# A transformer block with two expert layers: where the first expert's rows are transposed, and how the chunk ahead of it is emptied

## The chip, the cores and the metric

The kernel runs on one core of one Trainium2 chip. The metric is the device time of one execution in microseconds (us). A core has five engines with queues of their own: TensorE (PE in the profile; its weight loads are shown as PEld), VectorE (DVE), ScalarE (ACT), GpSimd (POOL) and SyncE (SP), which here only issues transfers. Engines wait for one another through semaphores.

## The reference

The input is 4096 tokens of 256 numbers. The block is a feed-forward layer (FFN) at half weight, an attention layer, and the same FFN once more:

```
x = x + 0.5 * ffn(layernorm(x))
x = x + attention(layernorm(x))
x = x + 0.5 * ffn(layernorm(x))

# ffn, on its input r:
a       = layer_norm(r, attn_nw, attn_nb)
combine, dispatch = top1_gate(a, wg, capacity=512)     # 8 experts, one per token
expert  = gelu(dispatched(a) @ inter_w[e] + inter_b[e]) @ output_w[e] + output_b[e]
dense   = gelu(a @ res_inter_w + res_inter_b) @ res_output_w + res_output_b
coef    = softmax(a @ res_coef)
return dense * coef[0] + combined(expert) * coef[1] + r
```

An expert takes at most 512 tokens, the first ones that chose it. All of it is float32.

## The kernel before

**Tiling.** Tokens are worked on in chunks of 512 (four tiles of 128). Both kinds of MLP, the dense one on a chunk of tokens and an expert's on its 512 slots, are one routine, `Mlp` with `tensor_chunk`: for each of 8 slices `k` of the 1024 inner features there is `up(k)` (6 matmuls of 512 columns), GELU on ScalarE, written twice (`f_h` and the rounded `f_h_hi`), a subtraction on VectorE that makes the low part `f_h_lo` (`split_h`, L311), and `down(k)` (12 matmuls of 256 columns into four accumulators `f_down`). Every float32 operand is split into a high and a low part, and three products stand for one. `down` runs two slices behind `up`, so TensorE's order is up(k), down(k-2), up(k+1), down(k-1), and so on; at a chunk's end stand up(7), down(5), down(6), down(7), and at its beginning up(0), up(1), up(2), down(0), up(3).

**Order of the chunks.** In the first FFN six dense chunks are followed by the 8 experts and then by two dense chunks, in the second FFN seven dense chunks by the 8 experts and one dense chunk. The order on each engine is the order in which the Python program writes it. What is done beside a slice is given as a dictionary from `k` to a list of functions (`beside`); on VectorE they follow `split_h(k)`, on ScalarE the GELU of slice k, on TensorE `down(k)`. The key `EARLY` on TensorE stands just ahead of up(2).

**Towards the experts.** During the fourth dense chunk (`mlp(3, ...)` on VectorE) each token's expert and slot are found: `choose`, `choose_one`, `place`, then `address` (six small instructions, the row addresses) and `weigh` (three, the gate's weight). After `weigh` GpSimd scatters all tokens to `slots_in` in memory with 32 indirect transfers (L580). When all have landed, SyncE loads the first expert's rows from there (`load_rows`, L397). VectorE reads their marks (`tokens_of`, L858 to L864), and TensorE transposes them (`turn_slots`, L1067, 8 small matmuls into `f_side`). ScalarE applies gain and shift (`slots_T`, L972, `f_aT`), and VectorE splits the result into `f_x_hi` (L273) and `f_x_lo` (L278), with which the expert's up(0) can begin. An expert's weights come as float32 and are split by VectorE, one slice at a time (`split_w`, L848 to L852, four instructions a slice), four slices ahead of use; for the first expert `first_weights(0)` to `first_weights(3)` are the first four. TensorE waits at each up(k) for the split of slice k.

**Emptying a chunk.** `empty` adds the bias to the four accumulators into the buffer `f_part` (L666) and adds `f_part`, scaled, to the tokens in `x_all` (L671). down(0) of the next chunk waits for the first of the two and for `split_h(0)`.

Of the kernel before, what the change touches and what calls it, by code (L numbers as in the profile page):

```python
# [35 lines left out]
NC = TOKENS // CH  # L36
# [363 lines left out]
def ffn_programs(nc, ctx, sems, mem, layer, x_tiles, x_in, res_w1, res_w2, res_b2, inter_w, output_w, output_b, slots_in,  # L400
# [3 lines left out]
    first_late = NC - LATE[layer]  # L404
# [7 lines left out]
    m = Mlp(nc, ctx, sems, tag)  # L412
# [196 lines left out]
    def vector(dve, beside=None, constants=None):  # L609
# [41 lines left out]
        def mix_of(a):  # L651

            dve.wait_ge(s["th_ready"], a + 1)
            v.tensor_scalar(c0[:, bass.ds(a * TT, TT)], th[:], 0.25, 0.25, ALU.mult, ALU.add)
            v.tensor_scalar(c1[:, bass.ds(a * TT, TT)], th[:], -0.25, 0.25, ALU.mult, ALU.add)

        def empty(c, turn):

            if turn > c:

                dve.wait_ge(s["stored"], 16 * TT * NE)
            if turn == 0:
                dve.wait_ge(s["b2_in"], 16)
            dve.wait_ge(m.down_done, turn * NK + NK)
            for t in range(TT):
                i = v.tensor_tensor(part[:, t, :], m.down_ps[t][:, 0:D], b2[:], ALU.add)  # L666
            i.then_inc(m.evacuated, 1)
            dve.wait_ge(m.evacuated, turn + 1)
            dve.wait_ge(s["x_made"], c + 1)
            for t in range(TT):  # L670
                i = v.scalar_tensor_tensor(x_all[:, c * TT + t, :], part[:, t, :], c0[:, c * TT + t:c * TT + t + 1],  # L671
                                           x_all[:, c * TT + t, :], ALU.mult, ALU.add)
            i.then_inc(s["updated"], 1)
# [31 lines left out]
        def rows_T(c):  # L705
            return aT_all[:, NC - 1 - c]

        def mlp(c, beside=None, turn=None):
            turn = c if turn is None else turn
            for k in range(NK):  # L710
                if k == NK - 1:
                    dve.wait_ge(s["aT_all_ready"], c + 2)
                    m.split_x_hi(dve, turn + 1, rows_T(c + 1))
                m.split_h(dve, turn, k, turn == 0)
                if k == NK - 1:
                    m.split_x_lo(dve, turn + 1, rows_T(c + 1))
                for f in (beside or {}).get(k, ()):
                    f()
            empty(c, turn)

        def mlp_before_experts(c, beside, after):

            for k in range(NK):
                m.split_h(dve, c, k, False)
                for f in beside.get(k, ()):
                    f()
            dve.wait_ge(s["e_aT_ready"], 1)
            m.split_x_hi(dve, c + 1, aT[:])
            m.split_x_lo(dve, c + 1, aT[:])
            for f in after:  # L730
                f()
            empty(c, c)

        def mlp_last(beside):
            for k in range(NK):
# [8 lines left out]
        def norms(c):  # L744

            a, b, d = c * 3 + 1, c * 3 + 2, c * 3 + 3
            at = {0: [lambda: stats_of(a)], 2: [lambda: logits_of(d - 3), lambda: y_of(a)], 3: [], 4: [],
                  5: [lambda: logits_of(a)], 6: [lambda: mix_of(d - 3)]}
            if c:
                at[0].insert(0, lambda: mix_of(a - 3))  # L750
                at[4].append(lambda: mix_of(b - 3))
            if b < NC:
                at[3].append(lambda: stats_of(b))
                at[4].append(lambda: y_of(b))
                at[5].append(lambda: stats_of(d))
                at[7] = [lambda: logits_of(b), lambda: y_of(d)]
            else:
                at[7] = [lambda: logits_of(NC)]
            return at
# [72 lines left out]

        mlp(1, norms(1))
        mlp(2, norms(2))
        mlp(3, {0: [lambda: mix_of(NC - 1), choose], 1: [choose_one], 3: [place], 4: [address], 5: [weigh]})
        for c in range(4, first_late - 1):
            mlp(c)

# [15 lines left out]
        def tokens_of(e):  # L854

            dve.wait_ge(feed.rows_in, (e + 1) * 16)
            marks = feed.rows[:, :, D]
            v.tensor_copy(weight[:], feed.rows[:, :, D + 1])  # L858
            v.tensor_scalar(vacant[:], marks, 0.0, None, ALU.is_equal).then_inc(s["token_chain"], 1)
            dve.wait_ge(s["token_chain"], e * 2 + 1)  # L860
            v.scalar_tensor_tensor(vacant[:], mem["spare"][:, 0:TT], 1.0, vacant[:], ALU.add,
                                   ALU.mult).then_inc(s["token_chain"], 1)
            dve.wait_ge(s["token_chain"], e * 2 + 2)
            v.scalar_tensor_tensor(token[:], marks, -1.0, vacant[:], ALU.add, ALU.add).then_inc(s["token_read"], 1)  # L864

        def expert(e, parity, first=False, last=False):
            c = e + first_late
            for k in range(NK):
                if k == 4:
                    dve.wait_ge(s["token_read"], e + 1)  # L870
                    if not first:
                        dve.wait_ge(s["stored"], e * 16 * TT)
                    v.tensor_copy(weight_now[:], weight[:])
                    v.tensor_copy(to[:], token[:]).then_inc(s["to_ready"], 1)
                    if not last:
                        dve.wait_ge(s["to_ready"], e + 1)
                        tokens_of(e + 1)
                following = rows_T(first_late) if last else aT[:]
                if k == NK - 1:
                    if not last:  # L880
                        dve.wait_ge(s["e_aT_ready"], e + 2)
                    m.split_x_hi(dve, c + 1, following)
                m.split_h(dve, c, k, False)
                if k == NK - 1:
                    m.split_x_lo(dve, c + 1, following)
                if not (last and k + W_AHEAD >= NK):

                    if not (first and k + W_AHEAD < W_RING):
                        dve.wait_ge(m.down_done, c * NK + (k + W_AHEAD - W_RING + 1))
                    split_w(e, k + W_AHEAD)  # L890
            dve.wait_ge(m.down_done, c * NK + NK)
            dve.wait_ge(eb2_in[parity], (e - parity) * 8 + 16)
            for t in range(TT):
                i = v.tensor_tensor(part[:, t, :], m.down_ps[t][:, 0:D], eb2[:, parity, :], ALU.add)
            i.then_inc(m.evacuated, 1)
            dve.wait_ge(m.evacuated, c + 1)
            for t in range(TT):
                i = v.tensor_scalar(part[:, t, :], part[:, t, :], weight_now[:, t:t + 1], None, ALU.mult)
            i.then_inc(s["done_ready"], 1)

        def first_weights(k):
            if k == 0:
                dve.wait_ge(s["scattered"], 16 * NT)
            split_w(0, k)

        mlp_before_experts(first_late - 1, {6: [lambda: first_weights(0), lambda: tokens_of(0)], 7: [lambda: first_weights(1)]},
                           [lambda: first_weights(2), lambda: first_weights(3)])
        expert(0, 0, first=True)
        with dve.Fori(0, NE // 2 - 1) as i:
            expert(i * 2 + 1, 1)  # L910
            expert(i * 2 + 2, 0)
# [76 lines left out]
    def tensor(pe, beside=None, constants=None):  # L988
# [72 lines left out]
        def turn_slots(e, first=False):  # L1061
            pe.wait_ge(feed.rows_in, (e + 1) * 16)
            if not first:
                pe.wait_ge(s["e_aT_ready"], e)
            for kd in range(KD):
                for t in range(TT):
                    i = nc.tensor.transpose(m.side[kd][:, t * P:(t + 1) * P], feed.rows[:, t, kd * P:(kd + 1) * P],  # L1067
                                            mem["id32"][:])
            i.then_inc(s["e_turned"], 1)
# [6 lines left out]
                return (lambda kd: ew1[0][:, r, kd, :]), (lambda kd: ew1[1][:, r, kd, :]), ew2[0][:, r, :], ew2[1][:, r, :]  # L1076
            m.tensor_chunk(pe, e + first_late, expert_weights, False, None if last else {EARLY: lambda: turn_slots(e + 1)})

        m.tensor_chunk(pe, first_late - 1, weights, False, {6: lambda: turn_slots(0, True)})
        with pe.Fori(0, NE - 1) as e:  # L1080
            expert(e)
        expert(NE - 1, last=True)
        for c in range(first_late, NC):
            m.tensor_chunk(pe, c + NE, weights, False, (beside or {}).get(c), last_layer and c == NC - 1)

    return Programs(sync, gpsimd, vector, scalar, tensor, s, m)


# [693 lines left out]
```

## Time and profile before

| | us |
|---|---|
| three runs: median | 1217.13 |
| three runs: lowest to highest | 1215.64 to 1217.16 |
| the profiled execution's own time | 1215.53 |
| its span (first to last instruction) | 1213.8 |
| TensorE busy with matmuls | 1175.2 (97%) |
| VectorE busy | 901.7 (74%) |
| ScalarE busy | 686.2 (57%) |
| GpSimd busy | 273.4 (23%) |

The profiled execution was 1.6 us faster than the median of the three runs, and its time is 1.7 us longer than its span. Times of instructions below are counted from the span's start. The dense chunk ahead of the first expert ends at 166 us in the first FFN and at 998 us in the second.

### The profile page before, as it was taken

What the parts mean: (1) busy time and instruction counts of PE and PEld (TensorE: products, weight loads), DVE (VectorE), ACT (ScalarE), POOL (GpSimd) and SP (SyncE); (2) the same over time, 40 slices, a digit from 0 to 9 for tenths busy, and PEclk for the clock granted to TensorE, in tenths of its full rate; (3) what the DMA queues carried; (4) which work ended last, traced back from release to release, by engine and by line L of the source; (5) the groups of instructions that cost most, each with busy time, mean ns of one, the idle gap of its engine ahead of it and who ended that gap; (6) DMA issues with size and microseconds to landing.
All of it is one profiled execution on the core that took longest, in us unless ns stands there. A gap on an engine that the chain in (4) does not pass through costs nothing. (4 is left out here: it accounts for less than half of the span.)

```text
span 1213.8 us, 28464 instructions
## 1 busy us (share of the span) xinstructions
PE 1175.2 (97%) x11133; PEld 874.6 (72%) x11133; DVE 901.7 (74%) x1963; ACT 686.2 (57%) x998; POOL 273.4 (23%) x322
## 2 busy tenths in 40 slices
PE   7999999999999989999999999978999999999998
PEld 6888889999989744434353443437888888999987
DVE  6867468888867877878779877567866459788874
ACT  4554445445454567786867778755455445554443
POOL 4651711121131000000000000014624600322422
PEclk9999999999999999999999999999999999999999
DMA  9702224344203633230442121007103514555622
GB/s 284 210 1 98 99 93 160 123 150 159 91 31 94 101 67 63 43 65 2 88 72 45 28 41 32 2 14 184 36 26 106 174 53 147 129 154 132 137 56 53
DMA packets 144992, 110.58 MB, mean 91 GB/s; under 512 B 73132, under 2 KB 132856, under 8 KB 144888
## 3 DMA queue, kind: packets, MB, share of 16 engines
q1 hardware_dynamic: 135672, 92.27, 29.0%
q0 software_dynamic: 9216, 16.85, 6.0%
q8 instruction: 74, 1.21, 0.4%
q14 instruction: 30, 0.25, 0.1%
HBM read 57.59 MB, written 34.73 MB: 76 GB/s over the span
## 5 line engine op out<-in xcount | busy, mean ns | idle before, releaser
L301 ACT ACTIVATE f_h<-f_up,vecT 128x512 f32<-128x512 f32 x256 | 176.5, 689 | 379.5 <-PE f_up L290 370.9
L1538 ACT ACTIVATE a_probs<-a_S 128x1024 f32<-128x1024 f32 (+3 forms) x320 | 272.9, 900 | 68.5 <-PE a_S L1431 35.0
L311 DVE TENSOR_TENSOR f_h_lo<-f_h,f_h_hi 128x512 fp32r<-128x512 f32 x256 | 176.2, 690 | 136.2 <-ACT f_h_hi L301 135.6
L1721 DVE TENSOR_TENSOR a_probs<-a_probs 128x2048 f32<-128x2048 f32 (+2 forms) x78 | 147.5, 1891 | 39.9 <-ACT a_probs L1538 37.9
L301 ACT ACTIVATE f_h_hi<-f_up,vecT 128x512 fp32r<-128x512 f32 x256 | 174.7, 682 | 0.0
L322 PE MATMUL f_down<-f_ew_hi,f_h_hi 128*128 128x256 f32 x512 | 143.3, 280 | 3.3 <-DVE f_h_lo L311 3.3
L322 PE MATMUL f_down<-f_w_hi,f_h_hi 128*128 128x256 f32 x512 | 145.3, 284 | 0.7 <-DVE f_h_lo L311 0.7
L1448 PE MATMUL a_cx<-a_probs,a_V 128*32 128x512 f32 (+3 forms) x1280 | 144.7, 528 | 0.4 <-DVE a_dd L1699 0.4
L324 PE MATMUL f_down<-f_w_hi,f_h_lo 128*128 128x256 f32 x512 | 144.8, 283 | 0.0
L323 PE MATMUL f_down<-f_w_lo,f_h_hi 128*128 128x256 f32 x512 | 144.7, 283 | 0.0
L323 PE MATMUL f_down<-f_ew_lo,f_h_hi 128*128 128x256 f32 x512 | 142.9, 279 | 0.0
L324 PE MATMUL f_down<-f_ew_hi,f_h_lo 128*128 128x256 f32 x512 | 142.6, 278 | 0.0
L1427 PE MATMUL a_S<-a_QT,a_early_keys 128*32 128x512 f16 (+3 forms) x1792 | 122.8, 359 | 3.5 <-ACT a_probs L1538 3.5
L1427 PEld LDWEIGHTS a_S<-a_QT,a_early_keys 128*32 128x32 f16 x1792 | 40.2, 95 | 93.2 <-ACT a_probs L1538 44.4
L322 PEld LDWEIGHTS f_down<-f_ew_hi,f_h_hi 128*128 128x128 f32 x512 | 96.3, 188 | 8.4 <-DVE f_h_lo L311 4.1
L322 PEld LDWEIGHTS f_down<-f_w_hi,f_h_hi 128*128 128x128 f32 x512 | 97.9, 191 | 5.5 <-DVE f_w_lo L769 1.5
L323 PEld LDWEIGHTS f_down<-f_w_lo,f_h_hi 128*128 128x128 f32 x512 | 97.7, 191 | 3.8
L323 PEld LDWEIGHTS f_down<-f_ew_lo,f_h_hi 128*128 128x128 f32 x512 | 96.1, 188 | 4.4
L324 PEld LDWEIGHTS f_down<-f_w_hi,f_h_lo 128*128 128x128 f32 x512 | 97.7, 191 | 0.0
L324 PEld LDWEIGHTS f_down<-f_ew_hi,f_h_lo 128*128 128x128 f32 x512 | 96.2, 188 | 0.0
L290 PE MATMUL f_up<-f_x_hi,f_w_hi 128*128 128x512 f32 x256 | 86.0, 417 | 6.0 <-DVE f_x_hi L273 4.9
L580 POOL DMA_INDIRECT slots_in<-f_y_all,f_scatter_at x64 | 66.9, 1046 | 75.0 <-issue 75.0
(201 smaller groups left out, 2168.4 us busy)
## 6 DMA issues: line engine op xcount, KB each, us to landing
f_aT_all<-in_L_ffn_inter_w SPq DMA_DIRECT2D x32, 512.0 KB, 4.0
f_aT_all<-in_L_ffn_output_w SPq DMA_DIRECT2D x32, 512.0 KB, 4.9
slots_in<-f_zeros SPq DMA_DIRECT2D x16, 516.0 KB, 13.2
f_aT_all<-slots_in SPq DMA_DIRECT2D x16, 516.0 KB, 4.3
out<-x_all SPq DMA_DIRECT2D x9, 512.0 KB, 3.4
x_all<-in_L_attn_x SPq DMA_DIRECT2D x8, 512.0 KB, 9.5
moe_rows<-f_zeros SPq DMA_DIRECT2D x8, 512.0 KB, 8.5
a_moe<-moe_rows SPq DMA_DIRECT2D x6, 512.0 KB, 4.2
```

Of the source, the lines that this page charges most:

```text
L290: last = nc.tensor.matmul(bank[:], w(kd), xs[:, kd, :], start=(n == 0), stop=(n == 3 * KD - 1))
L301: i = self.nc.scalar.activation(to, self.up_ps[k % UP_BANKS][:], ACT.Gelu_apprx_tanh, bias=bias)
L311: nc.vector.tensor_tensor(lo, h, hi, ALU.subtract).then_inc(self.h_split, 1)
L322: nc.tensor.matmul(bank, hi, w2_hi, start=(k == 0), stop=False)
L323: nc.tensor.matmul(bank, hi, w2_lo, start=False, stop=False)
L324: last = nc.tensor.matmul(bank, lo, w2_hi, start=False, stop=(k == NK - 1))
L580: nc.gpsimd.indirect_dma_start(out=slots_in, out_offset=bass.IndirectOffsetOnAxis(ap=scatter_at[:, t:t + 1], axis=0), in_=y_all[:, t, :], ...
L1427: last = nc.tensor.matmul(S[hp][k:k + DH, i, lo:CH], KT[j // TT][:, h, j % TT * P + k:j % TT * P + k + DH], QT[:, c % 2, h, lo:CH], start= ...
L1448: last = nc.tensor.matmul(cx[G % 2][i * DH:(i + 1) * DH, lo:CH], V[:, v_tile(b * QC, j), h * DH:(h + 1) * DH], probs[:, q % P_RING, i, lo: ...
L1538: nc.scalar.activation(probs[:, q % P_RING, hp * 2:hp * 2 + 2, lo:CH], S[hp][:, :, lo:CH], ACT.Exp).then_inc(exp_done[hp], 1)
L1721: v.tensor_tensor(total, total, probs[:, (q + 1) % P_RING, :, lo:CH], ALU.add).then_inc(s["summed"], 1)
```

## The change

There are three edits, and all of them act in both FFNs.

1. On TensorE `turn_slots(0)`, the transposition of the first expert's rows, stands behind down(5) of the dense chunk ahead of it and no longer behind down(6).
2. On VectorE the emptying of that chunk is cut in two parts, `take` (the accumulators into `f_part`) and `put` (`f_part` into `x_all`), and both stand inside the first expert. Slice 0 there is now: `first_weights(2)`, `take`, `split_h(0)`, `first_weights(3)`, `split_w(0, 4)`. `put` stands ahead of `split_h(2)`. For the other chunks `empty` calls both in one go, as it was.
3. `weigh` follows `address` directly, beside slice 4 of the fourth chunk; it stood beside slice 5.

```diff
         def empty(c, turn):
+            take(c, turn)
+            put(c, turn)
+
+        def take(c, turn):
             if turn > c:
                 dve.wait_ge(s["stored"], 16 * TT * NE)
...
             for t in range(TT):
                 i = v.tensor_tensor(part[:, t, :], m.down_ps[t][:, 0:D], b2[:], ALU.add)
             i.then_inc(m.evacuated, 1)
+
+        def put(c, turn):
             dve.wait_ge(m.evacuated, turn + 1)
             dve.wait_ge(s["x_made"], c + 1)
...
-        def mlp_before_experts(c, beside, after):
+        def mlp_before_experts(c, beside):
...
             m.split_x_hi(dve, c + 1, aT[:])
             m.split_x_lo(dve, c + 1, aT[:])
-            for f in after:
-                f()
-            empty(c, c)
...
-        mlp(3, {0: [lambda: mix_of(NC - 1), choose], 1: [choose_one], 3: [place], 4: [address], 5: [weigh]})
+        mlp(3, {0: [lambda: mix_of(NC - 1), choose], 1: [choose_one], 3: [place], 4: [address, weigh]})
...
         def expert(e, parity, first=False, last=False):
             c = e + first_late
             for k in range(NK):
+                if first and k == 0:
+                    first_weights(2)
+                    take(c - 1, c - 1)
+                if first and k == 2:
+                    put(c - 1, c - 1)
...
                 m.split_h(dve, c, k, False)
+                if first and k == 0:
+                    first_weights(3)
...
-        m.tensor_chunk(pe, first_late - 1, weights, False, {6: lambda: turn_slots(0, True)})
+        m.tensor_chunk(pe, first_late - 1, weights, False, {5: lambda: turn_slots(0, True)})
```

The order on VectorE from the first expert's `f_x_hi` on, before (`f_ew_hi` and `f_ew_lo` are a slice of the expert's weights, `f_b` is the bias, `f_c` a token's coefficient):

```order
L273 CAST f_x_hi<-f_aT 128x1024
L278 TENSOR_TENSOR f_x_lo<-f_aT,f_x_hi 128x1024
L848 CAST f_ew_hi<-f_aT_all 128x256
L849 CAST f_ew_hi<-f_aT_all 128x256
L851 TENSOR_TENSOR f_ew_lo<-f_aT_all,f_ew_hi 128x256
L852 TENSOR_TENSOR f_ew_lo<-f_aT_all,f_ew_hi 128x256
L848 CAST f_ew_hi<-f_aT_all 128x256
L849 CAST f_ew_hi<-f_aT_all 128x256
L851 TENSOR_TENSOR f_ew_lo<-f_aT_all,f_ew_hi 128x256
L852 TENSOR_TENSOR f_ew_lo<-f_aT_all,f_ew_hi 128x256
L666 TENSOR_TENSOR f_part<-f_down,f_b 128x256 x4
L671 SCALAR_TENSOR_TENSOR x_all<-f_part,f_c,x_all 128x256 x4
L311 TENSOR_TENSOR f_h_lo<-f_h,f_h_hi 128x512
```

The same place of the changed kernel, up to the same first `f_h_lo` of the expert:

```order
L273 CAST f_x_hi<-f_aT 128x1024
L278 TENSOR_TENSOR f_x_lo<-f_aT,f_x_hi 128x1024
L852 CAST f_ew_hi<-f_aT_all 128x256
L853 CAST f_ew_hi<-f_aT_all 128x256
L855 TENSOR_TENSOR f_ew_lo<-f_aT_all,f_ew_hi 128x256
L856 TENSOR_TENSOR f_ew_lo<-f_aT_all,f_ew_hi 128x256
L670 TENSOR_TENSOR f_part<-f_down,f_b 128x256 x4
L311 TENSOR_TENSOR f_h_lo<-f_h,f_h_hi 128x512
```

One slice of weights and the four instructions into `x_all` are gone from ahead of the first `f_h_lo`. They stand behind it: the slice of weights at once, the four instructions (now L677) behind two more slices of weights and the second `f_h_lo`, as the next rows show.

The order on VectorE of the changed kernel a little further on, from the second `f_h_lo` to the third:

```order
L311 TENSOR_TENSOR f_h_lo<-f_h,f_h_hi 128x512
L852 CAST f_ew_hi<-f_aT_all 128x256
L853 CAST f_ew_hi<-f_aT_all 128x256
L855 TENSOR_TENSOR f_ew_lo<-f_aT_all,f_ew_hi 128x256
L856 TENSOR_TENSOR f_ew_lo<-f_aT_all,f_ew_hi 128x256
L677 SCALAR_TENSOR_TENSOR x_all<-f_part,f_c,x_all 128x256 x4
L311 TENSOR_TENSOR f_h_lo<-f_h,f_h_hi 128x512
```

Before, nothing stood there between the slice of weights and the third `f_h_lo`.

The order on TensorE at the end of the dense chunk, changed kernel, from the last of down(5) to the first of down(6) (`f_side` takes the transposed rows):

```order
L322 MATMUL f_down<-f_w_hi,f_h_hi 128x256
L323 MATMUL f_down<-f_w_lo,f_h_hi 128x256
L324 MATMUL f_down<-f_w_hi,f_h_lo 128x256
L1077 MATMUL f_side<-id,f_aT_all 128x128 x8
L322 MATMUL f_down<-f_w_hi,f_h_hi 128x256
L323 MATMUL f_down<-f_w_lo,f_h_hi 128x256
```

Before, the row of the 8 transposing matmuls (L1067 there) stood 12 matmuls later, between down(6) and down(7).

## Rows read from the trace of the kernel before

**Rows 1.** The page, 40 slices of the span: TensorE's granted clock in tenths.

```profile
PEclk9999999999999999999999999999999999999999
```

**Rows 2.** Chain that ended last, second FFN: start, us, what.

```profile
1002.95 1.34 DVE f_part L666 x4
...
1005.99 0.61 DVE f_h_lo L311
```

**Rows 3.** Timeline of TensorE, second FFN: start, us, instruction, count [idle before <-releaser].

```profile
996.05 1.04 PE L1067 MATMUL f_side<-id,f_aT_all 128*128 128x128 f32 x8
...
998.24 0.28 PE L324 MATMUL f_down<-f_w_hi,f_h_lo 128*128 128x256 f32 x1
999.35 0.73 PE L290 MATMUL f_up<-f_x_hi,f_ew_hi 128*128 128x512 f32 x2 [0.83 <-DVE f_x_hi L273]
...
1001.18 0.63 PE L290 MATMUL f_up<-f_x_hi,f_ew_hi 128*128 128x512 f32 x2
...
1002.58 1.04 PE L1067 MATMUL f_side<-id,f_aT_all 128*128 128x128 f32 x8
1003.37 0.71 PE L290 MATMUL f_up<-f_x_hi,f_ew_hi 128*128 128x512 f32 x2
...
1006.64 0.39 PE L322 MATMUL f_down<-f_ew_hi,f_h_hi 128*128 128x256 f32 x1 [1.64 <-DVE f_h_lo L311]
...
1008.16 0.63 PE L290 MATMUL f_up<-f_x_hi,f_ew_hi 128*128 128x512 f32 x2
```

**Rows 4.** Timeline of TensorE, first FFN.

```profile
163.69 1.04 PE L1067 MATMUL f_side<-id,f_aT_all 128*128 128x128 f32 x8
...
165.88 0.28 PE L324 MATMUL f_down<-f_w_hi,f_h_lo 128*128 128x256 f32 x1
...
175.81 0.63 PE L290 MATMUL f_up<-f_x_hi,f_ew_hi 128*128 128x512 f32 x2
```

**Rows 5.** Timeline of VectorE, first FFN.

```profile
166.25 0.69 DVE L273 CAST f_x_hi<-f_aT 128x1024 fp32r<-128x1024 f32 x1 [1.35 <-ACT f_aT L972]
166.98 1.23 DVE L278 TENSOR_TENSOR f_x_lo<-f_aT,f_x_hi 128x1024 fp32r<-128x1024 f32 x1
168.12 0.29 DVE L848 CAST f_ew_hi<-f_aT_all 128x256 fp32r<-128x256 f32 x1
...
170.52 1.41 DVE L666 TENSOR_TENSOR f_part<-f_down,f_b 128x256 f32<-128x256 f32 x4
171.96 1.67 DVE L671 SCALAR_TENSOR_TENSOR x_all<-f_part,f_c,x_all 128x256 f32<-128x256 f32 x4
173.55 0.68 DVE L311 TENSOR_TENSOR f_h_lo<-f_h,f_h_hi 128x512 fp32r<-128x512 f32 x1
174.16 0.29 DVE L848 CAST f_ew_hi<-f_aT_all 128x256 fp32r<-128x256 f32 x1
```

**Rows 6.** Timeline of ScalarE, first FFN.

```profile
164.77 1.45 ACT L972 ACTIVATE f_aT<-f_side,vecT 128x512 f32<-128x512 f32 x2 [2.48 <-PE f_side L1067]
169.30 0.69 ACT L301 ACTIVATE f_h<-f_up,vecT 128x512 f32<-128x512 f32 x1 [3.08 <-PE f_up L290]
```

**Rows 7.** Timeline of VectorE, first FFN: the marks of the loaded rows are read.

```profile
162.45 0.17 DVE L858 COPY f_weight<-f_aT_all 128x4 f32<-128x4 f32 x1 [1.06 <-DMA f_aT_all<-slots_in]
```

**Rows 8.** Line L397, the loads of an expert's rows.

```profile
DMA to landing us min/median/max: 3.6/4.3/6.8
```

**Rows 9.** Timeline of VectorE, fourth chunk of the first FFN.

```profile
111.20 0.68 DVE L311 TENSOR_TENSOR f_h_lo<-f_h,f_h_hi 128x512 fp32r<-128x512 f32 x1
111.81 0.41 DVE L829 TENSOR_REDUCE f_t<-f_ex 128x32 f32<-128x256 f32 x1
...
117.30 1.22 DVE L278 TENSOR_TENSOR f_x_lo<-f_aT_all,f_x_hi 128x1024 fp32r<-128x1024 f32 x1
```

**Rows 10.** Timeline of GpSimd, first FFN: three of the 32 scatters.

```profile
113.80 1.24 POOL L580 DMA_INDIRECT slots_in<-f_y_all,f_scatter_at  x1 [27.97 <-issue]
...
116.62 0.96 POOL L580 DMA_INDIRECT slots_in<-f_y_all,f_scatter_at  x1 [0.30 <-issue]
117.88 1.48 POOL L580 DMA_INDIRECT slots_in<-f_y_all,f_scatter_at  x1 [0.30 <-issue]
```

More of the change, by code:

```diff
@@ L904, in first_weights @@
             split_w(0, k)
-        mlp_before_experts(first_late - 1, {6: [lambda: first_weights(0), lambda: tokens_of(0)], 7: [lambda: first_weights(1)]},
-                           [lambda: first_weights(2), lambda: first_weights(3)])
+        mlp_before_experts(first_late - 1, {6: [lambda: first_weights(0), lambda: tokens_of(0)], 7: [lambda: first_weights(1)]})
         expert(0, 0, first=True)
```

## The prediction

> **What bounds the kernel now.** I began with the page: TensorE is busy for 97% of the span, and its clock is granted in full, the 2.4 GHz level, in every slice [rows 1]. So the time is TensorE's work plus the few stretches in which it stands still, and a change that leaves its matmuls as they are can only add or remove such stretches. The waits of TensorE name them; the chain that ended last shows the same ones as stretches in which it leaves TensorE. It leaves it around the first expert of an FFN: transposed rows, ScalarE, `f_x_hi`, `f_x_lo`, two slices of weights, the emptying of the accumulators, the update of `x_all`, `f_h_lo`, and only then back to a `down` matmul [rows 2]. I then read both engines' timelines there.
>
> Second FFN [rows 3]: the last matmul of the dense chunk starts at 998.24. These matmuls start every 0.12 us, so TensorE is free at 998.36, and up(3) of the expert starts at 1008.16, 9.80 us later. Its own work between the two is up(0), up(1), up(2), down(0) and one transposition of the second expert's rows. An `up` takes 1.40 (1001.18 to 1002.58), the transposition 0.79 (1002.58 to 1003.37), and `down` 12 x 0.12, about 1.40. That is 4 x 1.40 + 0.79 = 6.39, and 3.41 is idle:
> - up(0) starts 999.35 - 998.36 = 0.99 late, for `f_x_hi`;
> - up(0) takes 1001.18 - 999.35 = 1.83 instead of 1.40, since its fifth matmul waits for `f_x_lo`: 0.43;
> - down(0) would start at 1003.37 + 1.40 = 1004.77 and starts at 1006.64, for `f_h_lo`: 1.87. Of this I leave 0.08 for slower first weight loads behind the transposition, which stay;
> - down(0) then takes 1.52, a restart of 0.12.
>
> That is 3.33 us to be had. First FFN [rows 4]: from 165.88 + 0.12 = 166.00 to 175.81 it is 9.81, the same picture, 3.34 us. Both together are 6.67 us.
>
> **The change part by part.** I work it out in the first FFN, where everything is tightest.
>
> The transposition, one place sooner. TensorE's own sum is unchanged: 8 matmuls move across 12 others. They start at 163.69 - 12 x 0.12 = 162.25. Everything behind them moves by the same 1.44: ScalarE's two activations from 164.77 to 163.33 [rows 6], with 1.45 us of duration; it is free then, since it had been idle for 2.48 before them. `f_x_hi` moves from 166.25 to 164.81; VectorE was idle for 1.35 before it [rows 5], and the work ahead of it comes up to 0.6 sooner (below), so 1.44 is there. `f_x_hi` ends at 165.50, half a microsecond before TensorE is free at 166.00: the 0.99 is gone. `f_x_lo` starts 0.73 later (166.98 - 166.25), at 165.54, and ends at 166.77. The fifth matmul of up(0) comes at 166.00 + 4/6 x 1.40 = 166.93: the 0.43 is gone too, with 0.16 to spare.
>
> The emptying in two parts. Before the first `f_h_lo` of the expert there now stand, from 165.54 on: `f_x_lo` 1.14 (166.98 to 168.12), one slice of weights 1.20 (two of them take 168.12 to 170.52) and `take` 1.44 (170.52 to 171.96) [rows 5]. `f_h_lo` can start at 169.32. Its other input is ScalarE's: up(0) ends at 167.40, and the first GELU started 0.46 after up(1) (169.30 [rows 6]; up(1) at 168.84 by the same offset as 1001.18 in rows 3), so the pair runs from 167.86 to about 169.1. So `f_h_lo` is done at 169.32 + 0.68 = 170.00. TensorE gets to down(0) at 166.00 + 3 x 1.40 + 0.79 + 0.08 = 171.07. The 1.87 and the restart are gone, with a microsecond to spare. down(0) also waits for `take`, done at 169.3.
>
> What is displaced. VectorE then does a slice of weights (`first_weights(3)`, to 171.13; up(3) needs it at about 172.5), another (to 172.33), `f_h_lo` 1 (0.61, 173.55 to 174.16, so to 172.94; down(1) needs it at 173.9), a slice (174.14), `put` (1.59, 171.96 to 173.55, so to 175.73), `f_h_lo` 2 (done by 176.4; down(2) comes at 172.5 + 3 x 1.40 = 176.7). This is the narrowest place, 0.3 us. Behind it VectorE has 1.20 + 0.61 = 1.81 us of work for each 2.80 us of TensorE's and catches up by a microsecond a slice. Nothing is done twice: I cost it at 0, and at up to 0.6 in each FFN if the cover is gone there (0.3 of margin and as much again). Below zero it can't be.
>
> What else hangs on these. The second expert's rows are requested when the first one's are turned. TensorE came to them 1002.58 - 997.09 = 5.5 us after the first turn's end [rows 3] and now comes 5.4 after it, and did not wait; of all such loads the median is 4.3 and the longest 6.8 [rows 8]. Cost 0, at most 1.4. SyncE's load of the second expert's weights waits for the fourth split slice, which was done at 170.5 in the first FFN and now is at 171.1; it is wanted at slice 4, ten microseconds later. In the second FFN SyncE's store of the chunk waits for `put`, two microseconds later than now; behind it are queued the second half of those weights, which wait for the eighth split slice and so go later still. Cost 0.
>
> The rows for the earlier turn. The wait that edit 1 adds is TensorE's for the loaded rows, behind down(5), with down(6), down(7) and the whole expert queued behind it. In the second FFN they have lain there for long. In the first they land just in time: VectorE waited 1.06 for them and read at 162.45 [rows 7], which is 0.2 later than the new turn at 162.25. Here edit 3 counts: `weigh` started at 111.81 behind a `split_h` at 111.20 [rows 9], and starts at 111.20 now, 0.61 sooner. GpSimd's scatters had waited for it [rows 10], so rows land at about 161.8, 0.4 before they are wanted. The `split_h` that `weigh` overtakes is 1.1 later and is not needed on TensorE for three more. Cost 0; 0.2 if the scatters take up the 0.61.
>
> The scatters are where a rule speaks against the change. The scatter that began at 117.88, inside an `f_x_lo` subtraction of 117.30 to 118.52, took 1.48 us, while the one at 116.62 took 0.96 [rows 9, 10]. The Trainium skill (SBUF — State Buffer, the section "SBUF: two separate sides") says that VectorE and GpSimd share a port pair as an exclusive lock, which an instruction of either holds to its end, and that a transfer issued by GpSimd then stands and waits for its descriptors. The pair at 117.88 agrees, 0.52 longer for 0.64 of overlap; by the rule a shifted train would meet other subtractions, and one more such meeting would eat 0.5 of the 0.61 and leave a wait of about 0.1 in the sum.
>
> **The sum.** 3.33 + 3.34 = 6.67, less 0 to 1.2 for `f_h_lo` 2. The profiled execution goes from 1213.8 to 1207.1 of span and from 1215.53 to 1208.9 of time. The median of the runs shown was 1.6 above the profiled execution, so I forecast 1217.13 - 6.7 = 1210.4. I take the near end, since every place has its margin worked out from durations that repeat to 0.02 us between the two FFNs.
>
> **Rivals.**
> - A, VectorE becomes the wait (12%). `f_x_hi` doesn't come sooner, because rows or ScalarE are late; only the emptying helps. Then 0.99 and 0.43 stay, and `f_h_lo` 0 is done at 166.25 + 0.73 + 1.14 + 1.20 + 1.44 + 0.68 = 171.44, before down(0) at 172.5. Gain 1.87 - 0.08 + 0.12 = 1.9 in each FFN, 3.8 in all: 1213.3. Against it: the idle time of ScalarE and VectorE in rows 5 and 6.
> - B, the gain is given back (5%): later stretches (experts, attention, the last chunk) hang on something that the first expert doesn't move, as a transfer. Time 1217.1. Against it: from there on the chain is almost all TensorE, and no transfer has a fixed time.
> - C, slower (4%). The scatters stretch in the first FFN, by their meeting VectorE's subtractions. Each could be 1.48 - 0.96 = 0.52 longer, 32 of them 16.6 us; rows then land up to 16.6 later, TensorE waits 16.6 - 0.4 = 16.2 at the turn, and the time is 1217.1 + 16.2 - 6.7 = 1226.6. It decides from 7.1 us of lateness on; by the nearest rows only some of the scatters are long.
> - D, the change removes less, as the turn waits up to 1.4 us for the second expert's rows in each FFN (4%): 1213.2.
>
> My forecast has 75%.
>
> **How the numbers follow.** Three runs of one kernel spread by 1.5 us, and about 0.2% (2.4 us) is what can be told from no change. Faster by more than that: forecast, A, and D, 75 + 12 + 4 less 1 for their tails = 90%. Within it: B, and 1 of the tails, 6%. Slower: C, 4%. The range begins at 1208.6: the whole gain below the lowest run (1215.64 - 6.7 = 1208.9) and a little for noise. It ends at 1213.6, which holds A and D.
>
> **What would show it.** The 8 transposing matmuls start 1.4 us sooner than at 163.7 and 996.0, and no wait stands before them. up(0) of the first expert follows down(7) with no idle time and takes 1.40. `f_part` is filled ahead of the first `f_h_lo`, and down(0) follows up(2) without a wait. From the dense chunk's last matmul to up(3) it is 6.5 us instead of 9.8 in each FFN. The first scatter starts at 113.2. I am wrong if TensorE waits at the turn in the first FFN for rows, at down(2) for `f_h_lo`, or if the distance from the first expert's up(3) to the span's end (1213.8 - 1008.2 = 205.6) grows.

## The result, and the profile after

The changed kernel takes 1211.38 us, the median of 6 runs (1209.9 to 1212.19), and the kernel before 1216.95 beside it (6 runs, 1215.64 to 1217.71). The ratio is 0.9951, with an interval of 0.994 to 0.9961. It is faster by 5.6 us, where 6.7 were forecast, and the time lies inside the range; the interval holds gains from 4.7 to 7.3 us. The profiled execution of the changed kernel took 1212.19 us, with a span of 1210.4 and a mean granted clock of 0.993; the one of before had 0.997. Two later runs of the kernel before, at 1465 and 1312 us with clocks of 0.75 and 0.85, were in a slow state and are left out of every number below.

The page of the changed kernel, busy times and the granted clock in 40 slices:

```profile
PE 1177.2 (97%) x11133; PEld 876.4 (72%) x11133; DVE 901.9 (75%) x1963; ACT 686.1 (57%) x998; POOL 272.6 (23%) x322
PEclk9999999999999999999999999988999999999999
```

Two slices show an 8 where [rows 1] has 9s. I come back to them; first the places that were changed. Timeline of TensorE, first FFN (start, us, instruction, count):

```profile
162.17 1.03 PE L1077 MATMUL f_side<-id,f_aT_all 128*128 128x128 f32 x8
165.81 0.28 PE L324 MATMUL f_down<-f_w_hi,f_h_lo 128*128 128x256 f32 x1
165.92 0.63 PE L290 MATMUL f_up<-f_x_hi,f_ew_hi 128*128 128x512 f32 x2
167.31 0.63 PE L290 MATMUL f_up<-f_x_hi,f_ew_hi 128*128 128x512 f32 x2
168.70 1.04 PE L1077 MATMUL f_side<-id,f_aT_all 128*128 128x128 f32 x8
169.50 0.71 PE L290 MATMUL f_up<-f_x_hi,f_ew_hi 128*128 128x512 f32 x2
170.97 0.28 PE L322 MATMUL f_down<-f_ew_hi,f_h_hi 128*128 128x256 f32 x1
...
172.37 0.63 PE L290 MATMUL f_up<-f_x_hi,f_ew_hi 128*128 128x512 f32 x2
```

No row has a wait behind it. The rows are turned at 162.17, 1.52 sooner than in [rows 4]. The dense chunk's last matmul is followed by up(0) after 0.11 us, up(0) takes 167.31 - 165.92 = 1.39, and down(0) comes 1.47 after up(2). From 165.81 + 0.12 to up(3) it is 6.44 us; 9.81 were read before and 6.5 forecast. The second FFN, against [rows 3]:

```profile
993.29 1.04 PE L1077 MATMUL f_side<-id,f_aT_all 128*128 128x128 f32 x8
...
996.92 0.28 PE L324 MATMUL f_down<-f_w_hi,f_h_lo 128*128 128x256 f32 x1
997.04 0.63 PE L290 MATMUL f_up<-f_x_hi,f_ew_hi 128*128 128x512 f32 x2
...
1003.49 0.63 PE L290 MATMUL f_up<-f_x_hi,f_ew_hi 128*128 128x512 f32 x2
```

1003.49 - 997.04 = 6.45: the same. Together the two places give (9.81 - 6.44) + (9.80 - 6.45) = 6.72 us. VectorE of the changed kernel in the first FFN, against [rows 5, 7]:

```profile
161.23 0.16 DVE L862 COPY f_weight<-f_aT_all 128x4 f32<-128x4 f32 x1
...
165.46 1.23 DVE L278 TENSOR_TENSOR f_x_lo<-f_aT,f_x_hi 128x1024 fp32r<-128x1024 f32 x1
...
167.80 1.41 DVE L670 TENSOR_TENSOR f_part<-f_down,f_b 128x256 f32<-128x256 f32 x4
169.13 0.68 DVE L311 TENSOR_TENSOR f_h_lo<-f_h,f_h_hi 128x512 fp32r<-128x512 f32 x1
...
173.94 1.67 DVE L677 SCALAR_TENSOR_TENSOR x_all<-f_part,f_c,x_all 128x256 f32<-128x256 f32 x4
175.52 0.68 DVE L311 TENSOR_TENSOR f_h_lo<-f_h,f_h_hi 128x512 fp32r<-128x512 f32 x1
```

The marks are read at 161.23 without a wait (162.45 before, after 1.06). The first `f_h_lo` is done at 169.81, 1.16 ahead of down(0); the third at 176.20, while down(2) would come at 172.37 + 3 x 1.40 = 176.57: 0.37 to spare, 0.3 forecast.

So the two places gave what was forecast, and yet this execution is only 1215.53 - 1212.19 = 3.34 us faster than the profiled one of before. Matching each matmul with its like, TensorE is ahead by 3.4 us behind the first FFN, by 1.8 from 451 on, by 1.3 at the second FFN's start, by 4.7 behind its first expert and by 3.4 at the end. Three stretches gave back 1.7, 0.4 and 1.3, and none of them lies where an edit was made.

### The profile page after: what moved, and what is told of

Its sections match the earlier page's. It is cut to its first block and busy times, and to the rows that moved or that the text cites. A ratio compares the mean times of both kernels' runs of the same rounds, so it can differ in the third digit from the quotient of the medians.

```text
span 1210.4 us, 28464 instructions
## 1 busy us (share of the span) xinstructions
PE 1177.2 (97%) x11133; PEld 876.4 (72%) x11133; DVE 901.9 (75%) x1963; ACT 686.1 (57%) x998; POOL 272.6 (23%) x322
```

## The experiments

All were compared with the kernel before on the same chip. Three questions were open: whether each edit is worth what its terms say, how near the margins are, and who takes 3.3 us back.

**The kernel before, once more.** No edit.

> The kernel before, unchanged, once more, for the spread of its own runs and their granted clocks. Theory 1 (stretches of half clock fall differently in each execution, behind the same idle stretches of TensorE): its mean clock differs from run to run between about 0.992 and 0.997, and the runs with the lower clock are the longer ones, by 1 to 3 us; the profile of before, with 0.997 and 1215.53 us, was a lucky one. Rival (the change costs clock): every run of this kernel has 0.996 or more, while the changed kernel has 0.992 to 0.994.

1216.58 us, 11 runs; ratio 0.9995 (0.9986 to 1.0004). As the theory has it, the clocks go from 0.993 to 0.997, and the two runs at 0.993 are the longest (1217.91 and 1218.21), the four at 0.997 lie from 1215.82 to 1216.58. Its profile loses 0.7 over the experts of the second FFN against the profile of before, with the same code. Part of what is given back is thus a difference between executions.

**The earlier turn alone.**

```diff
-        m.tensor_chunk(pe, first_late - 1, weights, False, {6: lambda: turn_slots(0, True)})
+        m.tensor_chunk(pe, first_late - 1, weights, False, {5: lambda: turn_slots(0, True)})
```

> The kernel before with the first edit alone: the first expert's rows transposed behind down(5). Everything on VectorE from f_x_hi on moves by 1.44 us in each FFN, so 0.99 and 0.43 of idle time go, but the first f_h_lo still stands behind two slices of weights, f_part and x_all. Theory (the two edits add up): down(0) starts 1.44 sooner, gain 2.9 us in all, 1214.1 where before has 1217.0; TensorE waits about 1.8 us at down(0). Rival (the turn alone gives nothing, as the last wait is f_h_lo's with a fixed end): below 0.5 us.

1214.04 us, 8 runs; ratio 0.9973 (0.9963 to 0.9984). TensorE of this kernel, first FFN:

```profile
161.91 1.09 PE L1067 MATMUL f_side<-id,f_aT_all 128*128 128x128 f32 x8
...
172.57 0.39 PE L322 MATMUL f_down<-f_ew_hi,f_h_hi 128*128 128x256 f32 x1 [1.63 <-DVE f_h_lo L311]
```

The idle time ahead of up(0) is gone and the one ahead of down(0) stays. TensorE's lead over before grew by 1.33 us at the first place and by 1.45 at the second; the terms 0.99 + 0.43 say 1.42. In the first FFN TensorE lost 0.1 at the turn itself: VectorE, which waits for the same rows, read them at 161.89, and the turn started at 161.91.

**The emptying in two parts alone.** The changed kernel with the turn back behind down(6) and `weigh` back at slice 5.

```diff
-  {... 4: [address, weigh]}          {5: lambda: turn_slots(0, True)}
+  {... 4: [address], 5: [weigh]}     {6: lambda: turn_slots(0, True)}
```

> The second edit alone: the emptying in two parts and the later fourth slice of weights, the turn behind down(6) and the gate's weight at slice 5 as before. Theory: 0.99 and 0.43 of idle time stay at up(0), the wait at down(0) of 1.8 us goes: gain 1.9 us in each FFN, 3.8 in all, 1213.2. Rival (VectorE has no slack behind): some of it comes back at down(1) or down(2), gain below 2.5.

1214.47 us, 9 runs; ratio 0.9973 (0.9963 to 0.9982). The places gave 1.92 each, 1.9 forecast. The two edits add up: 1.33 + 1.92 and 1.45 + 1.92 are within 0.1 of the 3.36 us that both places gave in the changed kernel. The median is 2.6 us below before, not 3.8. The profiled execution (1215.54 us) shows 1.7 of loss near 425 and 1.4 over the late experts.

**`weigh` back at slice 5,** the rest as changed.

```diff
-  4: [address, weigh]
+  4: [address], 5: [weigh]
```

> The changed kernel without its third edit: the gate's weight is made beside slice 5 again. Theory: the scatters of the first FFN start 0.6 us later, rows land at about 161.8 where the turn comes at 162.2, so nothing or up to 0.3 us is lost: 1211.4 to 1211.7. Rival (the third edit is what makes the rows arrive in time): TensorE waits 0.5 us or more at the turn of the first FFN and the time is 1212 or more.

1210.84 us, 5 runs; ratio 0.9945 (0.9931 to 0.9958), beside 0.9949 (0.9934 to 0.9963) for the changed kernel, run again. Edit 3 brings nothing that the times can show; what it does to the scatters comes next.

**The changed kernel again.**

> The changed kernel once more, as the partner of the others of this group. Theory (the gain is 6.7 us in every pair of executions with equal mean clock, and the 1.1 us that the first measurement lacked came from its clocks): about 1210.2 with a mean clock of 0.994 to 0.997 and about 1212.0 with 0.993, against about 1217.0 and 1218.0 for the kernel before. Rival (the change itself costs 1 us later on): 1211.4 whatever the clock.

1210.64 us, 5 runs: 1209.84 to 1210.64 at a clock of 0.994, 1211.38 and 1211.69 below it, as the theory has it. The scatters, by line (operation, count | busy us, mean ns | idle before): of before, of the changed kernel's first profile, and of its second:

```profile
L580 POOL DMA_INDIRECT slots_in<-f_y_all,f_scatter_at x32 | 33.4, 1044 | 37.4 <-issue 37.4
```
```profile
L580 POOL DMA_INDIRECT slots_in<-f_y_all,f_scatter_at x32 | 32.8, 1024 | 36.8 <-issue 36.8
```
```profile
L580 POOL DMA_INDIRECT slots_in<-f_y_all,f_scatter_at x32 | 34.0, 1062 | 36.8 <-issue 36.8
```

The first scatter starts at 113.80, 113.09 and 113.28. With `weigh` back it is 113.85, and the row is that of before. The changed kernel's second profile began 0.5 sooner than before and spent 0.6 more in the scatters. Its rows were just in time; VectorE and TensorE there:

```profile
162.25 0.17 DVE L862 COPY f_weight<-f_aT_all 128x4 f32<-128x4 f32 x1 [0.78 <-DMA f_aT_all<-slots_in]
```
```profile
162.32 1.04 PE L1077 MATMUL f_side<-id,f_aT_all 128*128 128x128 f32 x8
```

0.07 us of margin and no wait, in place of the 0.4 forecast. The six profiles taken with `weigh` at slice 5 show 33.4 each, the seven with it at slice 4 show 32.7 or 32.8 four times and 34.0 three times. The difference is made at one scatter, the fourth, which starts together with an `f_x_lo` subtraction. The two rows in the changed kernel's first profile, and in its second:

```profile
117.21 0.96 POOL L580 DMA_INDIRECT slots_in<-f_y_all,f_scatter_at  x1 [0.30 <-issue]
117.19 1.28 DVE L278 TENSOR_TENSOR f_x_lo<-f_aT_all,f_x_hi 128x1024 fp32r<-128x1024 f32 x1
```
```profile
117.41 2.02 POOL L580 DMA_INDIRECT slots_in<-f_y_all,f_scatter_at  x1 [0.30 <-issue]
117.38 1.22 DVE L278 TENSOR_TENSOR f_x_lo<-f_aT_all,f_x_hi 128x1024 fp32r<-128x1024 f32 x1
```

In all four short trains that scatter starts 0.020 to 0.025 us behind `f_x_lo` and takes 0.96, and the subtraction takes 1.28; in all three long ones it starts 0.034 to 0.039 behind and takes 2.01 or 2.02, and the subtraction takes 1.22. With `weigh` at slice 5 it starts 0.57 to 0.59 inside the subtraction and takes 1.47 or 1.48 in all six. So edit 3 moves this scatter to a place where 0.01 us decides: the 0.6 us won at the start of the train become 1.2 at its end, or 0. The last scatter ends at 155.31 in the first profile, at 156.72 in the second and at 156.65 before. With the short train VectorE finds the rows there at 161.23; with the long one it waits for them until 162.25. The rule on the shared ports (the Trainium skill, SBUF — State Buffer, "SBUF: two separate sides") lets the instruction that comes first keep them to its end. The rows agree where a scatter begins well inside `f_x_lo`: 1.06 longer with 1.19 of the subtraction to go, 0.52 longer with 0.64. A scatter that begins ahead of a subtraction is not longer (116.62 in [rows 10], with an `f_h_lo` from 116.69). What decides between 0.02 and 0.03 us the rows do not show.

**The turn behind down(4),** to see what late rows cost.

```diff
-  {5: lambda: turn_slots(0, True)}
+  {4: lambda: turn_slots(0, True)}
```

> The changed kernel with the first expert's rows transposed one place sooner still, behind down(4) and so ahead of up(7). Theory (in the first FFN the rows land at about 161.2, and TensorE would come to them at 159.3): TensorE waits 1.5 to 2 us there with up(7) queued behind it, and 1.5 to 2 us are lost in the first FFN, none in the second, where rows have lain ready; 1212.3. That gives the price of one place when rows are late. Rival (rows are early enough, or the wait is made up behind): 1210.6.

1212.86 us, 10 runs, from 1210.42 to 1217.14; ratio 0.997 (0.9958 to 0.9982). TensorE at the turn:

```profile
160.18 1.09 PE L1077 MATMUL f_side<-id,f_aT_all 128*128 128x128 f32 x8 [1.24 <-DMA f_aT_all<-slots_in]
```

The wait is paid in full by everything behind it: the first FFN gave 1.7 in place of 3.4, the second 3.2. That is the 1.5 to 2 us of the theory. down(5) is the earliest place that the rows allow. The runs spread by 6.7 us, more than those of any other kernel here. The one profile shows the short train of scatters; a long one would make the rows 1.2 us later, which is not shown for any of the runs and would not explain the whole spread.

**`put` right behind `take`,** both ahead of the first `f_h_lo`.

```diff
                     take(c - 1, c - 1)
-                if first and k == 2:
                     put(c - 1, c - 1)
```

> The changed kernel with the update of x_all not cut off: both parts of the emptying stand ahead of the first f_h_lo again, while the fourth slice of weights stays behind it. Theory: f_h_lo 0 comes 1.6 us later, done at 171.3 where down(0) can start at 170.97, so TensorE waits 0.4 us there, 0.9 us in both FFNs: 1.0 us slower than the changed kernel. So most of what the second edit gives is the slice of weights and the overlap with the earlier turn, not the cut. Rival (the cut carries it): 3 us slower.

1212.57 us, 5 runs; ratio 0.9963 (0.9948 to 0.9977). VectorE, then TensorE:

```profile
169.40 1.67 DVE L677 SCALAR_TENSOR_TENSOR x_all<-f_part,f_c,x_all 128x256 f32<-128x256 f32 x4
170.99 0.68 DVE L311 TENSOR_TENSOR f_h_lo<-f_h,f_h_hi 128x512 fp32r<-128x512 f32 x1
```
```profile
171.73 0.38 PE L322 MATMUL f_down<-f_ew_hi,f_h_hi 128*128 128x256 f32 x1 [0.44 <-DVE f_h_lo L311]
```

`f_h_lo` is 1.86 later than in the changed kernel, which uses up the 1.16 of margin; down(0) starts 0.76 later, 0.15 of which this profile was behind already. The places gave 2.4 each in place of 3.4, so `put` ahead costs 0.9 us in each FFN: 0.7 up to up(3), and 0.2 at down(1), where the second `f_h_lo` is late too. The medians say 1.9 in all. That is twice the 1.0 that I expected, which counted about 0.4 at each down(0) and nothing at down(1), and less than the rival's 3. About half of the 1.9 that the second edit gives in an FFN hangs on the cut, the other half on the moved slice of weights.

**The marks of an expert one slice later.** This asks for the 1.3 us lost over the late experts. At slice 4 VectorE waits until the expert before has been stored.

```diff
-                if k == 4:
+                if k == 5:
                     dve.wait_ge(s["token_read"], e + 1)
```

> The changed kernel, with the block of small instructions that waits for the last expert's rows to be stored (f_weight_now, the addresses, the next marks) beside slice 5 of every expert instead of slice 4. Theory (in the second FFN VectorE waits 2.5 to 3.4 us there for the stores, and f_h_lo of slice 4, queued behind, is up to 0.4 us late for TensorE in some experts, 1.3 us in all in the profile of the changed kernel): VectorE's wait shrinks to below 0.6 and TensorE's distance over the experts of the second FFN is the same 23.27 us each; 0.7 to 1.3 us faster than the changed kernel. Rival (those delays are not this wait's): same time, and the distances keep growing by 0.2 to 0.4.

1209.52 us, 5 runs; ratio 0.9937 (0.9922 to 0.9952). VectorE's waits (line waited for: us, times, longest) of the changed kernel and of the kernel before run again:

```profile
DVE f_weight_now L882 <- DMA out<-f_part,f_to: 20.3, 7, 3.4
```
```profile
DVE f_weight_now L873 <- DMA out<-f_part,f_to: 20.0, 7, 3.4
```

With the marks at slice 5 one wait of 1.2 us is left of it. TensorE's turns in the chain, with the marks at slice 4 (changed kernel, second profile) and at 5:

```profile
1068.83 0.87 PE f_side L1077 x8
1092.28 0.87 PE f_side L1077 x8
1115.72 0.87 PE f_side L1077 x8
```
```profile
1068.73 0.87 PE f_side L1077 x8
1092.01 0.87 PE f_side L1077 x8
1115.27 0.87 PE f_side L1077 x8
```

23.45 us an expert against 23.27. The loop loses nothing any more: TensorE's lead over before stays at 5.7 from the second FFN's first expert to the end.

**The same on the kernel before.** The same line changed there.

> The kernel before with the wait for the stored rows beside slice 5 instead of 4. Theory (the loss over the experts of the second FFN belongs to this wait and was there before the change: 0.7 us in the second profile of the unchanged kernel, 0 in the first): 0.3 to 1.0 us faster than the kernel before, and the distance from one transposition to the next is 23.27 us for all experts. Rival (only the changed kernel runs into this wait): same time as before.

1216.11 us, 11 runs; ratio 0.9992 (0.9983 to 1.0001). 0.9 us, not told from nothing; the waits fall from 17.2 us to 1.2. The wait was there before the change. What it costs TensorE differs between executions: nothing in the first profile of before, against which this run's profile gains nothing over the experts, 0.7 in its second one, 1.3 and 1.1 in the two of the changed kernel, 1.4 with the emptying alone.

**More matmuls ahead of the second FFN.** This asks for the clock.

```diff
         turn(0)
-        if not last_layer:
-            keep_warm(16)
+        keep_warm(28 if last_layer else 16)
```

> The changed kernel with 28 extra small matmuls on TensorE in the idle stretch of 3.5 us between the first transposition of the second FFN and its first up. Theory (the lower clock at this place follows TensorE's idle time): fewer microseconds at half clock between 806 and 826 us, a mean clock of 0.995 or more in the profile, and up to 0.5 us gained, as up(0) and up(1) there run faster. Rival (the clock at this place is given by the earlier idle stretch in the attention's last step): clock and time as for the changed kernel.

1210.63 us, 5 runs; ratio 0.995 (0.9936 to 0.9965). The runs' clocks rise to 0.995 to 0.997, and the median shows no gain. In the profile TensorE's lead stays at 3.35 across the start of the second FFN, where it fell by 0.7 in the changed kernel's second profile; a gain of that size five runs can't tell. TensorE of this kernel:

```profile
813.80 1.73 PE L1054 MATMUL f_down<-id,ones 128*128 128x128 f16 x28
...
817.52 1.16 PE L290 MATMUL f_up<-f_x_hi,f_w_hi 128*128 128x512 f32 x2 [1.99 <-DVE f_x_hi L273]
```

The clock was full through the added matmuls, which stand in time that was idle, and fell to 0.50 at 817.55, behind 1.99 of idle time, just as up(0) began.

**Both together.** The marks at slice 5 and the added matmuls.

> The changed kernel with the wait at slice 5 and with the 28 extra matmuls at the start of the second FFN. Theory (the two are independent; the extra matmuls alone gave 0.0 us in time, within 0.5): 1209.5, as with slice 5 alone, about 7.6 us faster than the kernel before. Rival (fewer stretches at half clock give time back): 1208.5 to 1209.

1209.57 us, 5 runs; ratio 0.9937 (0.9924 to 0.9951). The same as the marks alone. The changed kernel with the marks at slice 5 is the fastest found.

## Why the prediction was right

**The terms.** Every step of the sum was seen where it was put: the turn 1.4 to 1.5 sooner and without a wait, up(0) without idle time, `take` ahead of `f_h_lo` 0, down(0) in time, 6.45 us where 6.5 were forecast, in both FFNs. The parts measured alone, 1.33 and 1.45 for the turn and 1.92 for the emptying, are the terms 1.42 and 1.9. Within the 0.43 I had read one thing too simply: `f_x_lo` made TensorE wait for only about half of it, the rest was two pairs of matmuls of up(0) that took 0.57 in place of 0.46. Both went with the wait.

**The median.** 5.6 was measured and 6.7 forecast. The difference goes with the clocks of the runs. I group 61 runs of before's code and the 11 of the changed kernel by their mean granted clock: at 0.992 to 0.993 the medians are 1218.14 (19) and 1211.77 (5), at 0.994 they are 1217.02 (19) and 1210.19 (6). The gains at like clock are 6.4 and 6.8. At 0.996 to 0.997 before has 22 runs, 1216.48, and the changed kernel none. The second measurement gave 1210.64 beside 1217.02, 6.4. This is a grouping and not a cause: the added matmuls raised the clocks of the runs and left the median where it was. Nor is the rival of the first experiment, that the change costs clock, ruled out, as 22 of 61 runs against none of 11 stand in the highest group; by before's own groups that is worth 0.5 us at 1216.48 against 1217.02.

**Rival A** fell with the turn (no wait for rows, `f_x_hi` in time). **C** fell with the scatters: 32.8 and 34.0 us in all, against 33.4; neither made the turn wait. The meeting with `f_x_lo` that it spoke of did happen, but only one scatter of the 32 was longer by as much as 1 us. **D**: the second expert's turn at 168.70 has no wait; it comes 5.5 us behind the first one's end, as before, where I had written 5.4. **B** was partly true and I had put it as all or nothing. The first execution gave back 3.4 of 6.7, through the clock and the stores.

**Rows.** Of the 0.4 us of margin, 0.07 was there in one execution and over 0.9 in the other (162.17 - 161.23). The term was costed at 0 to 0.2 and was 0, in part by luck: by the rows the 0.61 that edit 3 was to give were 1.2 or 0, according to the fourth scatter, and with the emptying and `weigh` as before TensorE did lose 0.1 at the turn. With the whole change it did not wait in either case, and edit 3 is worth nothing in time.

**The clock.** I had read the 9s of [rows 1] as full clock in every slice. A 9 is 90% or more, and the same trace has two stretches of half clock at the start of the second FFN, as the last section shows. The sum did not rest on it, since none lies at the places that were changed.

**The sign that I named.** I had written that I would be wrong if the distance from up(3) to the end grew. It did, from 205.6 to 1210.4 - 1003.5 = 206.9. The mechanism stood nevertheless: VectorE's wait for stored rows took the 1.3, and it is in the unchanged kernel too (17.2 us of waiting in one execution, 20.0 in the other); with the marks at slice 5 the distance is 1208.0 - 1002.4 = 205.6 again. The sign was badly chosen, since it wasn't checked against a second execution of before.

Open stays why the stores land later in some executions, and which half-clock stretches an execution gets. The place of the late experts' loss is shown by moving the marks; the clock's share was only read from rows and groups of runs.

## What to carry to other kernels

Where an engine is busy for 97% of the span, add up its idle stretches at one place, ask of each which instruction on the other engine stands ahead of what is waited for, and move only that; two such moves added up here to within 0.1 us. Split what stands ahead before moving it: with the update of `x_all` moved along, a quarter of the gain was gone. A sum of traced durations can be good to 0.1 us at its place while the whole moves by 1.5 us between executions: profile the kernel before twice, before a sign like "the rest doesn't grow" is trusted. A margin behind a train of transfers by GpSimd is not a number of the code: here 0.01 us between the starts of a scatter and of a subtraction made 1.2 us at the train's end. It has to be seen in more than one execution.

## What was not expected of the hardware

The granted clock fell to half, 1.2 GHz, in short stretches, and differently from one execution to the next. Windows (start and end, length, then busy us and instructions of PE, PEld, DVE, ACT and POOL, granted clock, DMA share, GB/s) of the changed kernel's first profile: TensorE ahead of and in the first stretch, and the two at the second FFN's start.

```profile
441.40:443.40 2.00, 0.00 (x1) 0.00 (x0) 1.93 (x5) 0.80 (x1) 0.00 (x0) 1.00 0.00 0
443.40:444.90 1.50, 1.46 (x12) 0.83 (x16) 1.47 (x2) 0.16 (x1) 0.00 (x0) 0.99 0.00 0
444.90:448.30 3.40, 3.40 (x44) 1.29 (x40) 3.37 (x4) 1.24 (x2) 0.16 (x1) 0.50 0.00 0
...
806.80:813.50 6.70, 5.04 (x22) 4.86 (x23) 4.91 (x9) 0.00 (x0) 0.00 (x0) 0.50 0.01 2
817.00:823.70 6.70, 4.08 (x10) 3.24 (x11) 3.67 (x4) 4.20 (x5) 0.00 (x0) 0.50 1.02 336
```

The same places of before. Its attention runs 3.4 us later, and its idle stretch of 2.04 lies at 444.9:

```profile
446.88 1.26 PE L1359 MATMUL a_misc<-a_wvp,a_yT 128*128 128x296 f32 x4 [2.04 <-DVE a_z L1642]
448.63 1.03 PE L1459 MATMUL a_dn<-a_probs,ones 128*32 128x512 f32 x8
```
```profile
444.90:448.30 3.40, 1.42 (x8) 0.80 (x12) 3.30 (x6) 0.86 (x2) 0.00 (x0) 1.00 0.00 0
448.30:451.70 3.40, 3.40 (x76) 1.56 (x72) 3.37 (x4) 2.46 (x4) 0.16 (x1) 1.00 0.00 0
806.80:813.50 6.70, 2.81 (x14) 2.54 (x15) 6.21 (x9) 0.25 (x1) 0.00 (x0) 0.81 0.01 2
```

The same idle stretch and the same matmuls behind it: with full clock 76 in 3.40 us, in the changed kernel 44, and the 8 of `a_dn` there:

```profile
445.47 1.93 PE L1469 MATMUL a_dn<-a_probs,ones 128*32 128x512 f32 x8
```

1.93 against 1.03. That stretch cost the 1.7 us. The changed kernel's second profile has no fall there. At the second FFN's start, where TensorE stands still for longer, the stretches of half clock last 3.41 and 3.41 us in before, 6.83 and 6.83 in the changed kernel's first profile and 13.65 at once in its second; the lead lost there is only 0.4 to 0.7 us, as TensorE has idle time there that takes up much of it (in before it is busy for 2.81 of the 6.70 us from 806.8 on).
